# The LSTM's output gate moved from ScalarE to VectorE, and the waits for filled inputs moved to the reductions

## The reference

```python
# L0: RNN
xW = einsum('ntd,dh->nth', x, Wx) + b
h = tanh(xW[:, t] + h @ Wh)                       # 1024 steps
# L1: a gated linear state-space scan over 64 states (softplus, tanh, decay), projected back to 512
# L2: LSTM
A = xW[:, t] + h @ Wh                             # 2048 columns, 1024 steps
i, f, o = sigmoid(A[:, 0:H]), sigmoid(A[:, H:2*H]), sigmoid(A[:, 2*H:3*H])
g = tanh(A[:, 3*H:4*H])
c = f * c + i * g
h = o * tanh(c)
# L3: a per-batch matrix (base + low rank, made from cond) applied to x
x = x + L0(x); x = x + L1(x); x = x + L2(x); x = x + L3(x)
```

## Time and profile before

| | |
|---|---|
| median of 3 runs | 3979.16 us (3974.48 to 3982.3) |
| the profiled execution | 3974.48 us |
| its span, first to last instruction | 3972.6 us |
| TensorE busy | 92% |
| VectorE busy | 82% |
| ScalarE busy | 44% |
| GpSimd busy | 20% |
| mean granted TensorE clock | 0.997 |

### The profile page before, as it was taken

One profiled execution on the slowest core, in us unless ns is written; L12 is line 12 of the kernel. 1 busy time (PEld: TensorE's weight loads), 2 busy tenths in 40 slices (PEclk: granted clock), 3 DMA queues, 4 the chain that ended last, 5 costly groups with the idle time before them and its releaser, 6 DMA issues.

```text
span 3972.6 us, 255717 instructions
## 1 busy us (share of the span) xinstructions
PE 3652.4 (92%) x110802; PEld 3080.0 (78%) x110802; DVE 3273.6 (82%) x19153; ACT 1752.1 (44%) x8244; POOL 774.8 (20%) x3624
## 2 busy tenths in 40 slices
PE   6899999999999999999999999999999999999875
PEld 4688788878888788888888888887888888877664
DVE  5588888888888888888888888888888888888766
ACT  4244444444444444444444444444444444444432
POOL 0122222222222222222222222222222222212111
PEclk9999999999999999999999999999999999999999
DMA  7100000000000000000000000000000000000000
GB/s 271 48 7 7 10 10 10 7 7 10 10 10 9 9 7 7 9 10 10 10 7 7 9 10 10 10 7 9 7 10 10 9 10 7 7 7 7 6 6 8
DMA packets 19109, 63.32 MB, mean 16 GB/s; under 512 B 3958, under 2 KB 4526, under 8 KB 14914
## 3 DMA queue, kind: packets, MB, share of 16 engines
q1 hardware_dynamic: 17692, 46.67, 3.7%
q10 hardware_dynamic: 294, 0.33, 0.0%
HBM read 38.48 MB, written 8.39 MB: 12 GB/s over the span
## 4 chain that ended last, share of the span: by engine, by line
DVE 55%; PE 38%; issue 4%; ACT 2%; DMA 1%; SPq 0%; ACTq 0%; DVEq 0%; POOL 0%; POOLq 0%
PE ps_lstm L1013 31%; DVE lstm_sums L738 19%; DVE lstm_arg L743 8%; DVE lstm_ig_fc L749 6%; DVE rnn_sums L847 5%; DVE lstm_gates_2c L754 5%; DVE lstm_h_parts L778 3%; DVE lstm_h_scaled L771 2%; DVE lstm_h_parts L774 2%; PE ps_rnn L1052 2%; PE ps_lstm_in_b L1094 2%; PE ps_ssm L1094 1%; PE ps_x L1149 1%; ACT lstm_tanh_c L495 1%; DVE rnn_h_parts L893 1%
## 5 line engine op out<-in xcount | busy, mean ns | idle before, releaser
L1013 PE MATMUL ps_lstm<-lstm_Wh_parts,lstm_h_parts 128*20 128x256 f16 x65472 | 1969.9, 273 | 270.1 <-DVE lstm_h_parts L778 257.7
L1013 PEld LDWEIGHTS ps_lstm<-lstm_Wh_parts,lstm_h_parts 128*20 128x20 f16 x65472 | 1543.4, 91 | 672.1 <-DVE lstm_h_parts L778 527.1
L486 ACT ACTIVATE lstm_gates_2c<-lstm_arg 128x32 f32<-128x32 f32 x2048 | 469.6, 229 | 1384.1 <-DVE lstm_arg L743 1384.1
L738 DVE STREAM_TRANSPOSE lstm_sums<-ps_lstm 128x256 f32<-128x256 f32 x2048 | 910.0, 444 | 199.8 <-PE ps_lstm L1013 164.1
L347 POOL COPY lstm_sums<-lstm_in 128x32 f32<-128x32 f32 x2048 | 423.6, 209 | 1783.0 <-DVE lstm_arg L743 1774.6
L1052 PE MATMUL ps_rnn<-rnn_Wh_parts,rnn_h_parts 128*20 128x128 f16 x32736 | 640.1, 220 | 38.0 <-DVE rnn_h_parts L893 35.7
L1052 PEld LDWEIGHTS ps_rnn<-rnn_Wh_parts,rnn_h_parts 128*20 128x20 f16 x32736 | 548.6, 92 | 76.0 <-DVE rnn_h_parts L893 56.5
L743 DVE TENSOR_REDUCE lstm_arg<-lstm_sums 128x32 f32<-128x96 f32 x2048 | 538.0, 263 | 35.2
L495 ACT ACTIVATE lstm_tanh_c<-lstm_gates_2c 128x8 f32<-128x8 f32 x2048 | 410.5, 200 | 254.2 <-DVE lstm_gates_2c L754 254.2
L774 DVE TENSOR_TENSOR lstm_h_parts<-lstm_o_scaled,lstm_tanh_c 128x8 f16<-128x8 f32 x2048 | 333.5, 163 | 154.7 <-ACT lstm_tanh_c L495 96.3
L509 ACT ACTIVATE rnn_h<-rnn_arg 128x16 f32<-128x16 f32 x1024 | 221.0, 216 | 524.3 <-DVE rnn_arg L852 524.3
(11 more groups left out here) (181 smaller groups left out, 2702.2 us busy)
## 6 DMA issues: line engine op xcount, KB each, us to landing
layer_plus_2I<-in_L_cond_w SPq DMA_DIRECT2D x16, 1024.0 KB, 5.8
out<-out_rows SPq DMA_DIRECT2D x128, 64.0 KB, 1.9
x_rows<-in_x SPq DMA_DIRECT2D x31, 256.0 KB
lstm_Wx<-in_L_cond_Wh SPq DMA_DIRECT2D x1, 4096.0 KB, 17.4
lstm_Wx<-in_L_cond_Wx SPq DMA_DIRECT2D x1, 4096.0 KB, 13.9
layer_plus_2I<-in_L_cond_Wh SPq DMA_DIRECT2D x1, 1024.0 KB, 9.2
rnn_Wx<-in_L_cond_Wx SPq DMA_DIRECT2D x1, 1024.0 KB, 11.3
lstm_in<-in_L_cond_w SPq DMA_DIRECT2D x1, 1024.0 KB, 10.3
```

The lines of the kernel that those rows point to most:

```text
L486: A.activation(gate[h][:, 0:G, :].rearrange("p g q -> p (g q)"), arg[h][:, :, :].rearrange("p g n -> p (g n)"), ACT.Tanh, scale=gate_scale ...
L738: return mark(V.transpose(tr[h][s % 2][:, :, 0:QC], psL[h][:, 0:HW].rearrange("p (g c) -> p g c", c=QC)))
L1013: ins = mm(psL[h][QC * j:QC * j + LO + NB, 0:HW], hls[:, k, :], whl[:, k, h, e, j, :], start=(k == 0 and e == 0), stop=(k == KB - 1 and e ...
```

## The change

The scaled output gate is computed by VectorE in place of ScalarE: for half 0 between `new_cell(0)` and the RNN's transpose, for half 1 behind `lo_part(0)`. The h parts wait for it by `vec_done`. The waits for GpSimd's fills no longer stand behind the h parts and ahead of the first transpose, but ahead of each reduction, as the first of its two waits; the RNN's likewise.

```diff
                 def gates(h, s): ...
-                def out_gate(h, s):
-                    act.wait_ge(S[f"lstm_gated{h}"], s + 1)
-                    A.activation(o_s[h][:, :], gate[h][:, 2, :], ACT.Copy, scale=H_SCALE, bias=H_SCALE)
...
                         gates(0, s)
-                        out_gate(0, s)
                         gates(1, s)
                         tanh_cell(0, s)
-                        out_gate(1, s)
                         tanh_cell(1, s)
...
                 def transpose(h, s):
-                    if s == 0:
-                        vec.wait_ge(S[f"lstm_in_ready{h}"], 1)
                     vec.wait_ge(S[f"lstm_mm{h}"], s + 1)
...
                 def reduce(h, s, at):
+                    vec.wait_ge(S[f"lstm_in_ready{h}"], s + 1)
                     vec.wait_ge(S["vec_done"], at)
...
-                def next_x_filled(h, s):
-                    if s + 1 < CT:
-                        vec.wait_ge(S[f"lstm_in_ready{h}"], s + 2)
-                def tanh_done(h, s):
+                def out_gate(h):
+                    return mark(V.tensor_scalar(o_s[h][:, :], gate[h][:, 2, :], 1.0, H_SCALE, ALU.add, ALU.mult))
+                def tanh_done(h, s, o_at):
                     vec.wait_ge(S[f"lstm_tanhc{h}"], s + 1)
+                    vec.wait_ge(S["vec_done"], o_at)
...
                 def transpose_rnn(s):
-                    vec.wait_ge(S["rnn_x_filled"], s + 1)
                     vec.wait_ge(S["rnn_mm"], s + 1)
...
                 def reduce_rnn(s, at):
+                    vec.wait_ge(S["rnn_x_filled"], s + 1)
                     vec.wait_ge(S["vec_done"], at)
...
                         new_cell(0, p_at)
+                        o_at = out_gate(0)
                         if w["rnn"]:
                             r_at = transpose_rnn(s)
                         p_at = products(1, s)
-                        tanh_done(0, s)
+                        tanh_done(0, s, o_at)
                         h_part(0, s)
-                        next_x_filled(0, s)
                         at = hi_part(0)
                         new_cell(1, p_at)
                         lo_part(0, s, at)
-                        tanh_done(1, s)
+                        o_at = out_gate(1)
+                        tanh_done(1, s, o_at)
                         hi_part(1)
-                        next_x_filled(1, s)
                         at = h_part(1, s)
```

## The result

The changed kernel takes 4140.14 us (median of 4 runs, 4138.58 to 4149.03) against 3980.73 us of the kernel before beside it. The ratio is 1.0407, with a 95% interval of 1.0387 to 1.0428: 159 us slower; the forecast was 4108 us, by a sum of +132. The profiled execution took 4143.03 us.

What follows compares the result with a forecast made beforehand. Bound: the LSTM step's loop through VectorE, TensorE waiting for lo_part(0) in 918 steps. Late waits 128.5, out_gate 4.6, TensorE-bound steps +1, chunk starts -2: +132 us on 3974.48, 4106.6, given as 4108; range 4080 to 4180.

Steps and rivals of the forecast that it cites:

- The bound: LSTM step loop of 3.62 us through VectorE; TensorE idles for lo_part(0) in 918 of 1,024 steps.
- ScalarE's out_gate is off the path: ScalarE's two out_gate instructions a step, 0.21 us each, leave its free time: gain 0.
- Two late separate waits, 128.5 us: At both LSTM reduces the late second wait becomes its own instruction: 0.07 us each, 0.14 a step, 918 steps.
- The rule that semaphores are free: Skill's rule, by which the reduces' added waits are free and the two added VectorE instructions are the whole cost.
- C: Rival: waits free, VectorE's out_gate uncovered, 0.08 us x 918 = 73 us, 4052 us; chance 0.05.
- D: Rival: waits free and VectorE's out_gate covered, between +5 and -2 us, 3977 us, no change; chance 0.05.
- E: Rival: reduce's waits free, removed wait before RNN transpose lets products(1) go earlier, 20 us faster, 3957; chance 0.03.
- B: Rival: late waits plus uncovered out_gate, RNN transpose blocking its whole 0.31 us: 78 us more, 4186; chance 0.09.
- other waits: h_part(0)'s wait on out_gate(0), 0 with bound 0.02 us; RNN waits -0.07 +0.07; chunk-start transposes 2 us gained.
- the chunk starts: Transposes at the 32 chunk starts lose their separate wait: 32 x 0.07 = 2 us gained for half 0.
- The added instructions' own work: VectorE's two added tensor_scalar: out_gate(0) 0.005 us a step, 4.6 us over 918 steps; out_gate(1) 0.
- the forecast's own range: Range for two late separate waits on the loop: 4088 (0.06 us each) to 4129 us (0.08); chance 0.78.

Runs made afterwards that it cites:

- the out_gate alone: Kernel before with out_gate on VectorE and the h parts waiting for it, filled-input waits left where they were: 4001.76 us, 1.0054.
- the early waits: Kernel before with four already-met second waits a step, in reduce, h_part and hi_part, nothing else changed: 3992.24 us, 1.0031.
- the out_gate without waits: Kernel before, ScalarE still making the gate, with the change's two tensor_scalar added on VectorE, results unread, no waits: 3977.13 us, 0.9992.
- the loop of 1,651: Kernel before with six one-element memsets a step in VectorE's idle time, making its loop 1,651 instructions, no added wait: 3989.55 us, 1.0019.
- the first experiment: Changed kernel with the two waits of each reduction, the RNN's too, in the other order, vec_done first: 4014.0 us, 1.0085.

## Why the prediction was right, and by what it was short

*The bound* was read rightly: the step's loop through VectorE is what grew, and TensorE's wait for `lo_part(0)` took up all of the loss. From transpose 0 to transpose 0, 906 of 1,023 steps are over 0.09 us longer than in the kernel before; the sum went by 918.

*ScalarE's out_gate is off the path*: right. 360 us less work on ScalarE brought nothing, and `products(1)` of the changed kernel starts 0.56 behind reduce 1 as before (747.68 to 748.24). The rule of the Trainium skill ("ScalarE: Activation LUTs", Rules for kernel authors) to put adds and multiplies on VectorE had no gain to make here.

*Two late separate waits, 128.5 us*: right. Measured twice, by the swap of two waits: 126 and 125 us; 0.137 us in the median step for 0.14.

*The rule that semaphores are free* (the Trainium skill, "VectorE: DVE Perf Modes", Rules for kernel authors: "Minimize op *count*, not sems"): here the runs say the reverse. Two more instructions a step, without waits, cost nothing (0.9992); the order of two waits costs 3.1%, four waits that were already met 0.3%, and a wait on the instruction directly in front some 4%. Rivals C, D and E, which need free waits, are out, and so is B: the RNN's transpose blocks 0.23 to 0.24 us, not 0.31.

*The step that was mis-sized* is "other waits". The forecast put the waits of the h parts for the out_gate at 0 and the moved early waits at -2, for the chunk starts; they measured 20 to 22 and +11.5. The added instructions' own work, for which +4.6 stood, measured 0. What I costed at nothing, "separate, but met earlier and taken while the tanh is awaited", is nothing in the median step and yet brought the gaps at every 128th VectorE instruction: some 30 us together. The median step was right and the mean was not.

*Shown*: early separate waits alone bring gaps and 10 us, the same added instructions without waits bring neither, and the gaps stand at every 128th place whatever stands there. The traces also say that the time is lost there. Take the 819 steps inside 13 passes of the loop, each less the same step of the kernel before, and less the median of these differences. What is left, summed over the steps in which such a place lies, is 23.5 us in the changed kernel, 15.1 with the out_gate alone, 12.1 with the filled-input waits alone in second place, 9.1 with the early waits, 0.0 with the out_gate without waits and 0.3 in the loop of 1,651.

*Shown too*: a DMA packet of instructions goes with each place. The page of the changed kernel, one pass of its loop of 1,647 instructions (1672.2 to 1917.2 us), and the 0.3 us from 749.2 to 749.5 us, with packets, MB and their share:

```profile
q14 instruction: 235, 1.93, 0.2%
...
q14 instruction: 13, 0.11, 0.1%
...
q14 instruction: 1, 0.01, 7.9%
```

That the time fell into the range owes something to luck: the gaps weren't in the forecast, 4140 lies above the top of the forecast's own range (4129), and the stated range held it because it had been widened for rival B, which is false.

The start is worth a remark: the first LSTM transpose came 6.9 us later than before in the profiled execution. The granted clock over the first 190 us reads 0.90 there and 0.95 in the kernel before. But start and clock don't follow each other closely in the other variants (only 1.8 us later at 0.90 in the first experiment), so I can't assign it.

## What to carry to other kernels

Where an instruction needs two waits, write first the one that will come true last: it then rides on the instruction. The other becomes a separate one, which costs 0.07 us more if it is late; early, it costs nothing in a normal step, but here such waits brought 10 to 20 us a kernel by the gaps. Look for such instructions on the wait lines of the trace before and after an edit; a step that is right in the median can still hide a loss in a few steps, so compare the sum over all steps as well. Moving work from an idle engine to the one on the path costs by its dependencies more than by its instructions: ask what waits for it and how soon behind it.

## What was not expected of the hardware

Gaps of 0.1 to 0.4 us at every 128th instruction of VectorE, in some kernels and not in others with loops as long, 10 to 30 us a kernel. An 8,192-byte instruction packet starts 0.7 us behind each. A small VectorE instruction without waits takes 0.07 us of the queue, though its own duration reads 0.17; one that waits for the instruction directly in front starts 0.20 behind it.
